# A two-layer graph kernel on one core: the search runs four tiles further ahead, and the neighbour lists are made four rounds earlier

## What is computed

```python
# layer 0: of each node's neighbours, the 25 with the lowest numbers
vals, idx = top_k(where(A != 0, -arange(N), -inf), 25)
agg = max over k of X[idx]            # relu'd where the degree is at most 25
x = layernorm(x + relu(concat[X, agg] @ W0 + b0))
# layer 1: attention over all neighbours, 8 heads of 32
Wh = x @ W1;  e = leaky(s1[i] + s2[j] + edge_emb[adj])
alpha = softmax over the neighbours; h = alpha @ Wh
x = layernorm(x + elu(layernorm(h) * gamma + beta))
```

## Time and profile before

| what | us |
|---|---|
| three executions | 3190.37, 3209.11, 3204.43 |
| their median | 3204.43 |
| the profiled execution's own time | 3204.28 |
| its span | 3202.6 |
| DVE busy | 2501.0 |
| POOL busy | 2280.8 |
| PE busy | 2098.0 |
| ACT busy | 1218.3 |

### The profile page before, as it was taken

How to read it: one execution, slowest core, us unless ns; L and a number is a source line. 1 busy time by engine, 2 the same in 40 slices (tenths; PEclk the granted TensorE clock), 3 DMA queues, 4 the chain that set the end, 5 groups by cost and what they waited for, 6 DMA issues and landing times.

```text
span 3202.6 us, 30987 instructions
## 1 busy us (share of the span) xinstructions
PE 2098.0 (66%) x7199; PEld 1505.5 (47%) x7203; DVE 2501.0 (78%) x5719; ACT 1218.3 (38%) x2779; POOL 2280.8 (71%) x2376
## 2 busy tenths in 40 slices
PE   7446566865566666767677777766676756568565
PEld 2224334643344444555455555544454544356454
DVE  5697677888787887788888898889886776567776
ACT  3223334443344334434444444423332322224334
POOL 3276476677777777777777777777777777777774
PEclk9767676877677788887878878888888967779887
DMA  6676667766666667777777777766655545445443
GB/s 231 213 240 230 220 227 252 236 224 202 206 226 220 221 212 238 237 229 238 243 230 251 241 233 243 218 187 201 189 160 143 161 125 141 126 132 165 125 129 100
DMA packets 271980, 644.16 MB, mean 201 GB/s; under 512 B 67505, under 2 KB 170930, under 8 KB 245170
## 3 DMA queue, kind: packets, MB, share of 16 engines
q0 software_dynamic: 111360, 309.05, 32.7%
q1 hardware_dynamic: 160434, 333.08, 30.4%
HBM read 572.07 MB, written 69.86 MB: 200 GB/s over the span
## 4 chain that ended last, share of the span: by engine, by line
POOL 39%; DVE 20%; issue 17%; PE 13%; DMA 4%; DVEq 4%; ACT 3%; SPq 0%; POOLq 0%; ACTq 0%
POOL ring L728 37%; DVEq L1169 4%; PE score_p L985 4%; DVE pay L1217 3%; DVE agg L1398 3%; PE lin_p L1020 3%; PE att_p L1057 2%; DVE ring L1537 2%; DVE agg L1388 1%; DMA sorted_d<-srt 1%; DVE pick L1277 1%; DVE adj_h L1204 1%; ACT adj_i L797 1%; PE wh_p L1036 1%; PE lin_p L1018 1%
## 5 line engine op out<-in xcount | busy, mean ns | idle before, releaser
L728 POOL DMA_INDIRECT ring<-table_d,idx x1096 | 1055.0, 963 | 364.1 <-issue 331.1
L1057 PE MATMUL att_p<-ring,ident 128*128 128x256 f32 (+1 forms) x2384 | 655.3, 438 | 311.4 <-ACT x_t L835 227.8
L728 POOL DMA_INDIRECT ring<-sorted_d,idx x685 | 677.1, 989 | 208.7 <-issue 206.0
L1057 PEld LDWEIGHTS att_p<-ring,ident 128*128 128x128 f32 (+1 forms) x2384 | 518.8, 222 | 449.3 <-issue 286.0
L728 POOL DMA_INDIRECT ring<-in_x_dram,idx x411 | 396.5, 965 | 257.4 <-DVEq L1343 125.2
L1398 DVE TENSOR_REDUCE agg<-ring 128x256 f32<-128x2560 f32 (+9 forms) x120 | 455.5, 3796 | 69.4 <-DMA ring<-sorted_d,idx 51.2
L1020 PE MATMUL lin_p<-w_s,h_t 128*128 128x256 f32 x1024 | 412.5, 573 | 0.0
L985 PE MATMUL score_p<-pay,pick 128*128 128x322 f32 x1024 | 344.7, 485 | 27.5 <-DVE pick L1277 19.1
L1020 PEld LDWEIGHTS lin_p<-w_s,h_t 128*128 128x128 f32 x1024 | 278.6, 285 | 115.4 <-issue 61.2
L866 ACT ACTIVATE neg<-z 128x256 f32<-128x256 f32 x128 | 53.4, 417 | 725.5 <-DVE z L1440 725.4
L1537 DVE TENSOR_TENSOR ring<-ring,score_p 128x1536 f32<-128x1536 f32 (+10 forms) x128 | 320.7, 2505 | 9.8 <-issue 0.3
(11 more groups left out here) (200 smaller groups left out, 3357.1 us busy)
## 6 DMA issues: line engine op xcount, KB each, us to landing
adj_i<-in_adj_dram SPq DMA_DIRECT2D x208, 1024.0 KB, 5.8
sorted_d<-srt SPq DMA_DIRECT2D x128, 161.0 KB, 6.4
ring<-table_d,idx POOLq DMA_INDIRECT x1096, 2.9
pay<-in_x_dram SPq DMA_DIRECT2D x32, 512.0 KB
xs<-sorted_d SPq DMA_DIRECT2D x128, 128.0 KB
fin_d<-res SPq DMA_DIRECT2D x112, 128.0 KB, 5.8
fin<-fin_d SPq DMA_DIRECT2D x28, 512.0 KB, 6.8
out_dram<-turned_out SPq DMA_DIRECT2D x112, 128.0 KB
```

Of the source, the lines that this page charges most:

```text
L728: pool.indirect_dma_start(out=to[:, k * width:(k + 1) * width], out_offset=None, in_=source, in_offset=bass.IndirectOffsetOnAxis(ap=idx_at ...
L1057: last = pe.matmul(att_p[:, 0:C], ident[0:on, :], r3[0:on, s, 0:C], start=(s == 0), stop=(s == k - 1))
```

## The change

Two constants change. The prologue has 27 steps and searches tiles 0 to 26; round r searches tile r + 27 where it searched tile r + 23. `DAHEAD` is computed from `AHEAD` and goes from 42 to 46, so the degree casts stand in rounds 2 to 81. The lists of graphs 1 to 7 are made at the end of the rounds 16b - 8 and 16b - 6. The lists of graph 0 stay in the prologue's steps 17 and 18, and the rounds of both layers stay as they are.

```diff
 LATER = T + 7
-AHEAD = T + 7
-IDX_LEAD = (4, 2)
+AHEAD = T + 11
+IDX_LEAD = (8, 6)
 LAG0 = 9
 LAG1 = 5
 ROUNDS = TILES + LATER + 4
```

## The result

The kernel after took 3253.49 us (median of four runs, 3249.54 to 3259.18), the kernel before beside it 3203.11 (four runs). The ratio is 1.0164, with a 95% interval of 1.0129 to 1.0199: slower by 41 to 64 us, 50 in the medians. The profiled execution took 3249.54 us with a span of 3247.8, so 45.2 us more span than before.

A forecast was written before the change was run, and what follows sets the result against it. The rounds (DVE, PE, ACT, SP's stores) set the time up to 630.6 us, POOL from 640 us on. Terms 23.8 + 11.7 + 9.4 - 3.1 = +41.8 us gave 3246 us, range 3214 to 3267.

The forecast's parts named there:

- the last wait for a slot: Sign: POOL's last wait for a ring slot before its unbroken stretch, near 672 us instead of 630.6.
- The prologue, +23.8: Ahead of the first layer: inserted tiles 23 to 26 cost one more group of four, +23.8 us.
- POOL's stop before tile 4: In graph 0's gathers: POOL stands still 7.4 us for tile 0's ring slots, off the path.
- The second stream, +11.7: Rounds 5 to 8: adjacency loads and degree casts starting at round 2, not 6, slow this group, +11.7 us.
- the handover: Where POOL takes over from the rounds in setting the time, 630.6 us in the kernel before.
- The price of a load: Adjacency loads on SP: 4.4 us per 1 MB by the skill, so two fit in a round; 11.7 us less.
- Graph 2's list, +9.4: Graph 2's first list moves from after round 28 to after round 24, onto the chain: +9.4 us.
- The second list: Graph 2's shorter list, after round 26 beside PE's part of the chain: 0, up to 9.4 us in the range.
- Graph 1's lists, 0: Made after rounds 8 and 10, not 12 and 14: POOL's 22.2 us wait goes, but off the chain, 0.
- The codes, -3.1: Graph 3's codes, made in round 20 instead of 24: DVE's wait behind the attention matmuls goes, -3.1 us.
- After the handover, 0: After 630.6 us POOL has the same gathers to issue, and later lists and codes cost nothing: 0.
- the waits inside the rounds close up: Rival, 170 to 640 us: DVE's waits for ACT and PE shrink by 27 to 40 us; 3206 to 3219, chance 0.1.

The follow-up runs named there:

- the probe of round 24: The kernel before with 20 reduces of a constant tile, each with a drain, added on DVE at the end of round 24: 3221.96 us, ratio 1.0034.

## Why the prediction was right

It held in sign, in time (3253 against 3246, inside the range) and in place: the last wait for a slot was forecast near 672 us and came at 670.2. The forecast change of 41.8 us lies at the lower end of the measured 41 to 64. By its steps:

- **The prologue, +23.8: right within the scatter.** The three kernels with the longer prologue took 27.5 (the kernel after), 23.0 and 24.2 us more up to L1523 of round 0. They differ at the mark of tile 27, which stood behind ACT for 5.4, 2.3 and 1.4 us: ACT waited for a sorted store before it could copy and cast. The forecast had no such wait. POOL's stop before tile 4, forecast at 7.4 us, came at 11.3, 6.3 and 7.3.
- **The second stream, +11.7: right where it was priced, too large at the end.** Its group gained 11.1 us in the kernel after and 12.3 alone. The step took every us up to the handover as paid in full. That was wrong: 7.3 to 9.7 arrived in the run that changed only the stream. In the run with only the search ahead all that lies between L1523 of round 0 and the handover came out 655.43 - 212.05 - (630.58 - 189.08) = 1.9 us longer, where the stream and the codes were to give 11.7 - 3.1 = 8.6 (one execution of each kernel). Its rounds 9 to 12 were 5.4 us shorter than in the kernel before (56.2 against 61.6) and rounds 21 to 24 5.3. Why the later groups give time back isn't shown.
- **The price of a load.** The estimate of 4.4 us, from the Trainium skill ("DMA: Bandwidth & Descriptors", section "Anatomy of one DMA"), would have made the stream free. That section is on DMAs that GpSimd issues, and these loads are SP's: they took 5.5 us in the run that changed only the stream. Two of that length also fit in a round of 12 us or more, and the group became slow all the same. So the time of a single load doesn't decide this, at either price.
- **Graph 2's list, +9.4: measured 611.68 - 602.26 = 9.4**, in front of that very reduce, and 9.0 to 9.5 up to the handover. The second list was rightly taken at 0. "Its load has landed by then" was not so: DVE waited 0.9 us for it, and the chain now runs over that load.
- **Graph 1's lists, 0:** the run with these alone early shows nothing else.
- **The codes, -3.1:** the wait shrank from 3.1 to 1.5 us only. That stretch gained 8.1 us in all, most of it time that the later groups give back.
- **After the handover, 0:** 5.6 us more in the profile. Four other kernels whose work there is nearly the same (the search ahead with late lists, with graph 1's early, the early stream, the probe of round 24) lie at 2569 to 2580 us, so this is within their scatter.

The rival that the waits inside the rounds close up is out: DVE's waits for ACT's roots and PE's permutations were 33.8 + 19.9 = 53.7 us before, and 39.4 + 14.4 = 53.8 in the kernel after.

That 41.8 meets the 39.6 of the handover so closely is in part luck: this execution's prologue was 3.7 us dearer than forecast, and what followed up to the handover 5.9 us cheaper (12.1 instead of 18.0). The reason given for the last step was too simple. That the lists in POOL's stretch cost nothing fits a room of about 11 us in the ring, which DVE's lateness may use up; it isn't that DVE's work is free there.

## What to carry to other kernels

A wait that a change removes is worth something only if the chain goes through it; here the kernel before had a wait of 22 us and the slower kernel after had none. Four more steps of prologue were paid in full (23 to 27.5 us), so run ahead only as far as the latest list needs; but one step fewer won nothing that the time shows. And "engine X is the bound" may mean no more than that the others have the room of the buffer between them: price added work against that room, in us, and not against the busy share. And before a difference of a few us in a stretch is explained, compare two executions that do the same work in it: here they were up to 5 us apart.

## What the runs showed of the hardware

A gather's issue on POOL takes longer beside some of DVE's instructions. In the kernel before, the timelines of POOL and DVE show one such pair:

```profile
258.16 1.51 POOL L728 DMA_INDIRECT ring<-in_x_dram,idx  x1 [0.30 <-issue]
```

```profile
258.19 0.66 DVE L1277 TENSOR_TENSOR pick<-rank,count 128x512 f32<-128x512 f32 x1
```

Laid over each other for the whole run, 210 of the 2256 gathers meet a pick, a float32 tensor_tensor with both inputs in SBUF. These last 0.17 us more than the usual 0.95 in the mean, and make 36.0 of the 56.0 us that all gathers together last beyond it. The 182 that meet a mark (L1204), a tensor_tensor of 1.2 us with one input in PSUM, last 0.00 us more. The Trainium skill ("SBUF — State Buffer", section "Who interferes with whom") says that a DVE instruction with two SBUF inputs contends with a GpSimd instruction that reads SBUF, and reports a probe in which tensor_tensor didn't stall DMAs issued from GpSimd; here, where each gather reads its indices from SBUF, the gathers beside one are longer. No run changed the picks, so this is seen in the overlap and not tested. In the kernel with the search 22 tiles ahead the same sum was 68.0 us, 47.8 of it beside picks. Twelve us more of issue where 9 were to be won would explain why that kernel gained nothing. But the sum varies by itself: in the kernel with work added at round 60, which has the same picks as the kernel before, it was 61.6 us, 43.6 beside picks. Whether the shorter lead or chance made it larger isn't shown.
